# Reordering the hand-over from the adapter stage to the expert tiles on four engine queues

## Chip, cores and metric

The kernel runs on one core of one Trainium2 chip. The metric is the device time of one execution in microseconds (us); the median of the timed runs counts.

## What is computed

Two layers over 4096 tokens (8 batches of 512) with 256 channels. Layer 0 adds to x a feed-forward net whose input is a low-rank adapter of x, chosen by a language id; its activations and weights are rounded to 8 bits. Layer 1 runs a per-language adapter with a layer norm over the rows, a router with 9 experts, and the two best experts of each token:

```python
x = x + L0_ffn(L0_cond(x, ids0, lora_A, lora_B, lang_embed), clips, w_gate, w_up, w_down)
y = L1_cond(x, ids1, W1, b1, W2, b2, gamma, beta)       # adapter, residual, layer norm
probs = softmax(y @ Wr); topk_w, topk_idx = top_k(probs, 2); topk_w /= sum(topk_w)
cw[token, topk_idx] += topk_w                           # 9 experts
gate = silu(einsum('th,ehi->tei', y, Wg))
out = einsum('tei,eih,te->th', gate * einsum('th,ehi->tei', y, Wu), Wd, cw)
return x + out
```

## The kernel before

Five engines run hand-written instruction lists, each in its own order: SP (which only issues DMAs), PE (TensorE), ACT (ScalarE), DVE (VectorE) and POOL (GpSimd). They meet only at named semaphores. What an engine does next is the next call in its list; a call whose semaphore is not yet there holds up all that stands behind it on that engine. The change moves calls inside these lists.

**Front part (0 to about 190 us).** The dense feed-forward net of layer 0, then the adapter of layer 1 in 16 steps of 256 tokens (ST = 16), two to a batch `b`. Per batch DVE computes router logits (`logits`), the two choices (`first_choice`, `second_choice`, which write one-hot masks `OH`), and later, when PE has summed the masks (`rank`), the place of each token in its expert's list (`positions`) and the payload columns (`payload`, which raises the semaphore `route`). `gain` and `affine` finish the normalised rows in `pay`, and SP stores them to the DRAM table `rows` (`store_rows`). PE's `adapter_out` of a step feeds that step's `gain` (line 1243); ACT's `squares` (line 898) follows the gain, DVE's `variance` (line 1220) follows both steps' squares, and ACT's `second_weight` (line 940) is needed by `payload`. For each batch POOL turns the places into 8 one-hot tiles (`slot_hot`, lines 1672 to 1680), raising `lh`.

**Hand-over (about 190 to 262 us).** It consists of these pieces.

- `order_experts` and `first_tiles` (lines 1352 to 1374, DVE) sort the experts by their load after six batches. The result `perm` is what SP's `load_piece` (lines 456 to 464) waits for: piece n is one of the matrices Wg, Wu, Wd (n % 3) of expert n // 3 in that order, 0.7 MB each.
- A piece must be split into two fp16 halves before PE can use it: ACT `piece_sum` (948, 950), PE `piece_top` (659), DVE `piece_scale` (1379 to 1386), ACT `piece_hi` (956), DVE `piece_lo` (1394).
- The rows of the first 5 tiles (SOLO = 5) are fetched early. DVE `hot_first` (1324) and PE `slots_first` (591) find which token sits in which slot, DVE `token_rows` (1341 to 1348) writes their indices (`it` = 1), and POOL's `gather` (1699) fetches the 128 rows of a tile by an indirect DMA.
- For the other 67 tiles the same is done with `table_counts` (1408 to 1430), `table_rows` (1435 to 1447), `hot_rest` (1324, two instructions of 2304 elements a partition), PE `slots_rest` (600), `token_rows` again (`rest_rows` after the change) and `table_experts` (1450 to 1458). `table_scales` and `unscale` (1461 to 1464, 1405) fill a table of scale factors. `slots_rest` needs all eight `slot_hot` (`lh` = 8), that is also the last batch's `payload`.

**Tiles.** 72 tiles of 128 slots. In tile t: ACT `x_hi` (961), DVE `x_lo` (1471), PE `turn_rows` (668), DVE `evac_rows` (1476), PE `proj(t, 0)` (689, 12 matmuls, gate), ACT `silu` (970), PE `proj(t, 1)` (12 matmuls, up), DVE `times` (1494), ACT `h_bound` (976), DVE `h_scale` (1500 to 1504), ACT `h_hi` (980), DVE `h_lo` (1510), SP `turn_hid` (472, a DMA transpose), PE `down` (740, 17 matmuls), DVE `finish` (1519), POOL `add_rows` (1731, indirect DMA that adds into `out`). `proj(t, 1)` waits for `times(t - 1)`, since both use one PSUM region; `proj(t, 0)` waits for `silu(t - 1)` in the same way.

PE also has `keep_busy(n, bank)`: n matmuls of 128x512 whose result nobody reads.

In the lists before the change, DVE's order between the loop over batches and the loop over tiles is: gain(15), order_experts, first_tiles, variance(7), positions(6), hot_first, payload(6), affine(13), logits(7), first_choice(7), token_rows(1, ...), second_choice(7), affine(12), piece_scale(0), piece_scale(1), piece_lo(0), x_lo(0), evac_rows(0), affine(15), positions(7), payload(7), affine(14), piece_lo(1), x_lo(1), table_counts, piece_scale(2), table_rows, piece_lo(2). POOL's order there is: gather(0) to gather(4), slot_hot(6), slot_hot(7), side(0), side(1). In the loop over tiles, iteration t handles times(t - 1) and prepares tiles t + 1 and t + 2:

```python
if t == 0:
    hot_rest(0)
if t == 1:
    hot_rest(1)
if t == 2:
    token_rows(2, SOLO, TILES - SOLO, it72)
    table_experts()
if t == 3:
    table_scales()
```

Of the kernel before, what the change touches and what calls it, by code (L numbers as in the profile page):

```python
# [9 lines left out]
NB = 8  # L10
# [26 lines left out]
SOLO = 5  # L37
# [4 lines left out]
def build_program(nc, xT, id0, id1, low, clips, wg, wu, wd, W1, b1, W2, b2, gam, bet,  # L42
                  LT, Wr, Wg, Wu, Wd, out):
    ctx = ExitStack()
    with ctx:
# [236 lines left out]
        def batch(of, b):  # L282
            if 0 <= b < NB:
                of(b)
# [246 lines left out]
        def _(e):  # L531
# [11 lines left out]
            def keep_busy(n, bank):  # L543
                for _ in range(n):
                    e.matmul(ps[:, bank, :], onesb, onesb.rearrange("p (a n) -> p a n", a=1).to_broadcast([P, 4, P]), start=True, stop=True)  # L545
# [26 lines left out]
            def rank(b):  # L572
                oh = OH[:, b % 2, :]
                w.wait_ge("pos", b)
                if b == last:
                    w.wait_ge("it", 1)
                w.wait_ge("xb", XB_UN)
                w.wait_ge("oh", b + 1)
                for t in range(5):
                    o = 9 * t if t < 4 else 64  # L580
                    for u in range(min(t + 1, 4)):
                        m = e.matmul(ps[:, 6, 128 + o:128 + o + 9], tri if u == t else onesb, oh[:, 9 * u:9 * u + 9],
                                     start=(u == 0), stop=(u == min(t, 3)))
                m.then_inc(S["rk"], 1)
# [66 lines left out]
            def piece_top(n):  # L651
                w.wait_ge("hsum", 2 * n + 2)
                if n == 0:
                    w.wait_ge("relu", ST)
                else:
                    w.wait_ge("hsc", sc_after(n - 1))
                if n == 3:
                    w.wait_ge("sq", ST)
                e.matmul(top(n), onesb, col(wsb, n), start=True, stop=True).then_inc(S["htopp"], 1)
# [148 lines left out]

            for b in range(NB + 1):
                step(dense_down, 2 * b)  # L810
                if b < NB:
                    batch(rank, b - 2)
                step(adapter_out, 2 * b - 1)
                if 0 < b < NB:
                    keep_busy(3, 1)
                step(adapter_in, 2 * b)
                step(dense_down, 2 * b + 1)
                step(logits_and_rows, 2 * b)
                if b < NB:
                    keep_busy(3, 0)  # L820
                step(adapter_in, 2 * b + 1)
                step(logits_and_rows, 2 * b + 1)
                step(adapter_out, 2 * b)
            keep_busy(6, 0)
            rank(last - 1)
            keep_busy(6, 0)
            slots_first()
            piece_top(0)
            piece_top(1)
            keep_busy(10, 0)  # L830
            rank(last)
# [5 lines left out]
            for t in range(TILES + 3):  # L837
                if 0 < t < TILES:
                    proj(t, 0)
                for n in pieces(t - 1):  # L840
                    piece_top(n)
                if 0 < t < TILES - 1:
                    turn_rows(t + 1)
                if 3 <= t <= TILES:
                    down(t - 3)
                if t == 2:
                    slots_rest()
                if 0 < t < TILES:
                    proj(t, 1)
                if t == TILES - 1:  # L850
                    turn_gated_hi(TILES - 2)
                    turn_gated_lo(TILES - 2)
                if t == TILES:
                    down_hi(TILES - 2)
                    turn_gated_hi(TILES - 1)
                    down_lo(TILES - 2)
                if t == TILES + 1:
                    turn_gated_lo(TILES - 1)
                    down_hi(TILES - 1)
                    down_lo(TILES - 1)  # L860

        @block.scalar
        def _(e):
# [88 lines left out]
            def piece_hi(n):  # L952
                if n >= 6:
                    w.wait_ge("slots", 2)
                w.wait_ge("hsc", sc_after(n))
                e.activation(halves_out(n)[0], slot_in(n), ACT.Copy, scale=col(wsc, n)).then_inc(S["hhi"], 1)  # L956
# [92 lines left out]
            piece_sum(0)  # L1049
            piece_sum(1)  # L1050
            piece_hi(0)
            second_weight(last)
            x_hi(0)
            piece_hi(1)
            piece_sum(2)
            x_hi(1)
# [25 lines left out]
        def _(e):  # L1082
# [246 lines left out]
                w.wait_ge("lh", 6)  # L1329
                same_tile(hot5, q16[:, 0:48], r16[:, 0:SOLO], 48, SOLO)  # L1330

            def hot_rest(k):
                w.wait_ge("slotF", 1)
                w.wait_ge("lh", 4 * k + 4)
                same_tile(hot72[:, 32 * k:32 * k + 32, :], q16[:, 32 * k:32 * k + 32], r16, 32, TILES)

            def token_rows(k, at_, n, tmp):
                v, low_, none_, both = tmp
# [227 lines left out]
            for b in range(-1, NB):  # L1566
                step(affine, 2 * b - 3)
                step(residual, 2 * b)
                step(gain, 2 * b - 1)
                step(clip_h, 2 * b + 1)  # L1570
                batch(positions, b - 2)
                batch(variance, b - 1)
                batch(payload, b - 2)
                step(affine, 2 * b - 4)
                step(residual, 2 * b + 1)
                batch(logits, b - 1)
                batch(first_choice, b - 1)
                step(clip_h, 2 * b + 2)
                batch(second_choice, b - 1)
                step(gain, 2 * b)  # L1580
            gain(ST - 1)
            order_experts()
            first_tiles()
            variance(last)
            positions(last - 1)
            hot_first()
            payload(last - 1)
            affine(ST - 3)
            logits(last)
            first_choice(last)  # L1590
            token_rows(1, 0, SOLO, it5)
            second_choice(last)
            affine(2 * last - 2)
            piece_scale(0)
            piece_scale(1)
            piece_lo(0, (0, 1))
            x_lo(0)
            evac_rows(0)
            affine(ST - 1)
            positions(last)  # L1600
            payload(last)
            affine(ST - 2)
            piece_lo(1, (0, 1))
            x_lo(1)
            w.wait_ge("pos", NB)
            table_counts()
            piece_scale(2)
            table_rows()
            piece_lo(2, (0, 1))
            w.wait_ge("route", NB)  # L1610
            w.wait_ge("ad", ST)
            for t in range(TILES + 3):
                if 0 <= t - 1 < TILES:
                    times(t - 1)
                if t == TILES:
                    evac_gated(t - 2)
                for n in pieces(t - 3):
                    if n in split:
                        piece_lo(n, (1,))
                for n in pieces(t - 2):  # L1620
                    piece_lo(n, (0,) if n in split else (0, 1))
                if 0 <= t - 1 < TILES:
                    h_scale(t - 1)
                if t + 2 < TILES:
                    x_lo(t + 2)
                if t + 1 < TILES:
                    evac_rows(t + 1)
                if t == TILES:
                    finish(t - 3)
                if 0 <= t - 1 < TILES:  # L1630
                    h_lo(t - 1)
                if t >= 3 and t != TILES:
                    finish(t - 3)
                if t == TILES + 1:
                    evac_gated(t - 2)
                for n in pieces(t - 1):
                    piece_scale(n)
                if t == 0:
                    hot_rest(0)
                if t == 1:  # L1640
                    hot_rest(1)
                if t == 2:
                    token_rows(2, SOLO, TILES - SOLO, it72)
                    table_experts()
                if t == 3:
                    table_scales()
                for n in range(3, 3 * E):
                    if max(begin[n] + 1, 3) == t:
                        unscale(n)

        @block.gpsimd
        def _(e):
# [118 lines left out]
            for b in range(NB):  # L1771
                batch(slot_hot, b - 2)
                power(b)
            for t in range(SOLO):
                gather(t)
            slot_hot(last - 1)
            slot_hot(last)
            side(0)
            side(1)
            for t in range(TILES + 3):  # L1780
                if 2 <= t < TILES + 2:
                    weigh(t - 2)
                if 2 <= t <= 3:
                    gather(2 * t + 1)
                    gather(2 * t + 2)
                if 4 <= t < TILES - 5:
                    gather(t + 5)
                if t >= 3:
                    add_rows(t - 3)
                if t + 2 < TILES:  # L1790
                    side(t + 2)
# [61 lines left out]
```

## Time and profile before

| what | us |
|---|---|
| runs | 658.28, 661.67, 664.20 |
| median | 661.67 |
| profiled execution, its own time | 658.28 |
| its span, first to last instruction | 656.6 |
| outside the span (658.28 - 656.6) | 1.7 |
| PE busy | 602.6 (92%) |
| DVE busy | 514.8 (78%) |
| ACT busy | 440.1 (67%) |
| POOL busy | 441.8 (67%) |

Starts are counted from the first instruction of the span. "Busy" leaves out waits and the issuing of DMAs. The granted clock is a share of TensorE's 2.4 GHz: 0.50 is 1.2 GHz, 1.00 is 2.4 GHz. A label of the form `<-X` beside an idle time names what the trace takes to have ended that wait.

### The profile page before, as it was taken

The page shows a single profiled execution, that of the slowest core. Times are in us where ns is not written, and L with a number is a line of the kernel's source. Part 1 is how long each engine was busy: PE and PEld are TensorE (multiplying, and loading weights), DVE is VectorE, ACT ScalarE, POOL GpSimd, SP SyncE. Part 2 cuts the span into 40 slices and gives each one's busy share as a digit, 9 for nine tenths or more (in the row PEclk, how much of TensorE's full clock was granted, in tenths as well). Part 3 has the DMA queues.
Part 4 walks back from the last instruction along what each step waited for, and adds up shares of the span by engine and source line. Part 5 has one row for each costly group of instructions (what it writes and reads, how often), then busy time and mean ns, then how long its engine had stood idle before and what let it go on. Part 6 is the DMA issues. An engine that isn't in the chain of part 4 may idle for free.

```text
span 656.6 us, 15688 instructions
## 1 busy us (share of the span) xinstructions
PE 602.6 (92%) x4478; PEld 412.7 (63%) x4482; DVE 514.8 (78%) x1361; ACT 440.1 (67%) x744; POOL 441.8 (67%) x597
## 2 busy tenths in 40 slices
PE   7998888999994487999999999999999999999995
PEld 2343335766762265677777777777777777777774
DVE  5579995899997887888888888888776666666653
ACT  3759995998964456888787787777665444555542
POOL 4116560187885986888888888878878677666544
PEclk8979999999996798999999999999999999999998
DMA  8522001346448238999898999978996666666552
GB/s 268 205 51 87 1 0 50 97 133 211 146 134 272 90 52 183 237 194 201 179 187 164 190 165 193 198 121 111 153 162 115 112 111 109 109 111 116 100 91 33
DMA packets 149378, 89.35 MB, mean 136 GB/s; under 512 B 106788, under 2 KB 142260, under 8 KB 149300
## 3 DMA queue, kind: packets, MB, share of 16 engines
q1 hardware_dynamic: 134596, 68.77, 47.0%
q0 software_dynamic: 14080, 19.54, 18.0%
q8 instruction: 44, 0.72, 0.5%
q14 instruction: 34, 0.28, 0.1%
q10 hardware_dynamic: 624, 0.03, 0.1%
HBM read 44.68 MB, written 18.40 MB: 96 GB/s over the span
## 4 chain that ended last, share of the span: by engine, by line
PE 51%; DVE 24%; issue 8%; DMA 7%; ACT 5%; SPq 2%; POOL 2%; POOLq 1%; DVEq 0%; ACTq 0%
PE ps L689 27%; PE ps L740 14%; DMA small<-small 3%; PE ps L545 2%; DVE big L1552 2%; DVE big L1394 2%; PE ps L668 2%; DVE small L1191 2%; DVE big L1201 1%; DVE small L1265 1%; PE ps L563 1%; PE ps L540 1%; DVE small L1243 1%; DVE small L1510 1%; DMA big<-in_Wu 1%
## 5 line engine op out<-in xcount | busy, mean ns | idle before, releaser
L689 PE MATMUL ps<-big,small 128*128 x1608 | 251.7, 313 | 1.9 <-ACT small L970 1.3
L689 PEld LDWEIGHTS ps<-big,small 128*128 128x128 f16 x1608 | 156.9, 98 | 80.4 <-issue 3.8
L1731 POOL DMA_INDIRECT out<-small x67 | 107.4, 1603 | 75.5 <-DVE small L1519 73.7
L740 PE MATMUL ps<-big,small 128*128 x1105 | 131.3, 273 | 0.6 <-DMA small<-small 0.6
L740 PEld LDWEIGHTS ps<-big,small 128*128 128x128 f16 x1105 | 105.2, 98 | 12.2 <-issue 1.0
L976 ACT ACTIVATE small<-small 128x704 f16<-128x704 f32 x67 | 52.6, 785 | 77.7 <-DVE small L1494 71.6
L1510 DVE SCALAR_TENSOR_TENSOR small<-small 128x64 f16<-128x64 f32 (+1 forms) x134 | 72.6, 583 | 20.5 <-ACT small L980 14.4
L1699 POOL DMA_INDIRECT small<-rows,small x67 | 75.8, 1131 | 11.8 <-issue 10.6
L1494 DVE SCALAR_TENSOR_TENSOR small<-ps,small 128x704 f32<-128x704 f32 x67 | 63.5, 947 | 25.0 <-issue 13.2
L980 ACT ACTIVATE small<-small 128x704 f16<-128x704 f32 x67 | 59.1, 882 | 28.0 <-DVE small L1504 28.0
L1707 POOL TENSOR_SCALAR small<-small 128x1 f32<-128x1 f32 x67 | 69.7, 1040 | 0.0
L1680 POOL TENSOR_SCALAR big<-small 128x128 f16<-128x128 f32 x64 | 61.3, 971 | 0.9
L1660 POOL TENSOR_TENSOR big<-small 128x512 f32<-128x512 f32 x24 | 31.6, 1315 | 44.7 <-ACT small L1028 44.7
L970 ACT ACTIVATE small<-ps,small 128x704 f32<-128x704 f32 x67 | 55.5, 829 | 0.0
L956 ACT ACTIVATE big<-big,small 128x1408 f16<-128x1408 f32 (+1 forms) x24 | 36.0, 1500 | 27.7 <-DVE small L1383 27.7
L1394 DVE SCALAR_TENSOR_TENSOR big<-big,small 128x704 f16<-128x704 f32 (+3 forms) x45 | 45.5, 1018 | 5.0 <-ACT big L956 3.8
L545 PE MATMUL ps<-small 128*128 128x512 bf16 x151 | 43.6, 425 | 1.4 <-POOL small L1736 1.4
L948 ACT ACTIVATE big<-big 128x1408 f16<-128x1408 f32 (+1 forms) x24 | 33.6, 1401 | 7.0 <-DMA big<-in_Wg 5.2
L1666 POOL TENSOR_TENSOR small<-small 128x4 f32<-128x4 f32 x8 | 8.3, 1040 | 44.5 <-DVE small L1220 44.5
L1519 DVE TENSOR_SCALAR small<-ps,small 128x256 f32<-128x256 f32 x67 | 36.0, 537 | 1.8 <-PE ps L714 1.7
L689 PE MATMUL ps<-big 128*128 128x352 f16 x120 | 23.4, 354 | 14.8 <-DVE big L1476 7.2
L1025 ACT ACTIVATE small<-ps,small 128x512 f32<-128x512 f32 x48 | 33.7, 806 | 3.9 <-PE ps L791 2.9
(266 smaller groups left out, 1068.5 us busy)
## 6 DMA issues: line engine op xcount, KB each, us to landing
big<-in_Wg SPq DMA_DIRECT2D x8, 704.0 KB, 6.2
big<-in_Wu SPq DMA_DIRECT2D x8, 704.0 KB, 8.4
big<-in_Wd SPq DMA_DIRECT2D x8, 640.0 KB
rows<-small SPq DMA_DIRECT2D x8, 518.0 KB, 5.0
big<-in_xT SPq DMA_DIRECT2D x8, 512.0 KB, 7.0
small<-in_xT SPq DMA_DIRECT2D x16, 256.0 KB, 4.5
out<-big SPq DMA_DIRECT2D x16, 256.0 KB, 4.3
small<-rows,small POOLq DMA_INDIRECT x67
```

The source lines that it names most:

```text
L545: e.matmul(ps[:, bank, :], onesb, onesb.rearrange("p (a n) -> p a n", a=1).to_broadcast([P, 4, P]), start=True, stop=True)
L689: m = e.matmul(ps[:, 2 * j + h, 0:352], xsT_(t)[:, 2 * xp + k, :], bigh[:, bass.ds(o + (4 * j + 2 * wp + k) * I + 352 * h, 352)], start=(n ...
L740: m = e.matmul(ps[:, 7, 0:H], hTE_(t)[:, hc_, :], bigh[:, bass.ds(o + 8 * I + (6 * wp + c) * H, H)], start=(n == 0), stop=(n == len(terms) ...
L970: e.activation(hid_(t).rearrange("p (a n) -> p a n", a=2), ps[:, 0:2, 0:352], ACT.Silu, scale=factor(t, 0)).then_inc(S["sg"], 1)
L980: e.activation(hh_(t)[:, 0:I], hid_(t), ACT.Copy, scale=hc_of(t)[:, 2:3]).then_inc(S["hhi2"], 1)
L1394: m = e.scalar_tensor_tensor(lo[:, a_:b_], slot_in(n)[:, a_:b_], col(wsc, n), hi[:, a_:b_], ALU.mult, ALU.subtract)
L1494: e.scalar_tensor_tensor(v, ps[:, 2:4, 0:352], factor(t, 1), v, ALU.mult, ALU.mult).then_inc(S["hid"], 1)
L1510: m = e.scalar_tensor_tensor(hh_(t)[:, o:o + b_ - a_], hid_(t)[:, a_:b_], hc_of(t)[:, 2:3], hh_(t)[:, a_:b_], ALU.mult, ALU.subtract)
L1680: m = e.tensor_scalar(lohot[:, 8 * b + i, :], ioP, slot8[:, i:i + 1], value[:, 4 * b + i % 4:4 * b + i % 4 + 1], ALU.is_equal, ALU.mult)
L1699: e.indirect_dma_start(out=xs_(t), out_offset=None, in_=Xs[0:512 * 6, :] if t < SOLO else Xs[:, :], in_offset=bass.IndirectOffsetOnAxis(ap ...
L1707: e.tensor_scalar(w_[:, 0:1], x_[:, 258:259], slotF[:, t:t + 1], 1.0, ALU.is_equal, ALU.subtract).then_inc(S["wc"], 1)
L1731: e.indirect_dma_start(out=out[:, :], out_offset=bass.IndirectOffsetOnAxis(ap=IT[:, t:t + 1], axis=0), in_=yw_(t), in_offset=None, compute ...
```

## The change

No instruction's shape is changed and no computing instruction is added or taken away; calls are moved within the lists of PE, ACT, DVE and POOL. SP's list stays.

- PE: `rank(6)` runs ahead of `adapter_out(15)`; the two keep_busy(6, 0) become one keep_busy(12, 0); `piece_top(0)` runs ahead of `slots_first`; `slots_rest` runs after `proj(1, 1)`, where it stood ahead of `proj(2, 1)`.
- ACT: `x_hi(0)` runs ahead of `second_weight(7)`.
- DVE: `order_experts` and `first_tiles` go into the last pass of the batch loop, ahead of `logits(6)`; the list behind the loop has a new order; `table_counts`, `table_rows` and both halves of `hot_rest` run together in iteration 0 of the tile loop, `rest_rows` and `table_experts` in iteration 1, `table_scales` in iteration 2.
- POOL: `slot_hot(6)` runs ahead of the five first gathers; `gather(5)` and `gather(6)` run in iteration 1, and so on to `gather(8)` in iteration 3.

```diff
 # PE
             for b in range(NB + 1):
                 step(dense_down, 2 * b)
-                if b < NB:
-                    batch(rank, b - 2)
+                batch(rank, b - 2)
                 step(adapter_out, 2 * b - 1)
...
-            keep_busy(6, 0)
-            rank(last - 1)
-            keep_busy(6, 0)
+            keep_busy(12, 0)
+            piece_top(0)
             slots_first()
-            piece_top(0)
             piece_top(1)
...
-                if t == 2:
-                    slots_rest()
                 if 0 < t < TILES:
                     proj(t, 1)
+                if t == 1:
+                    slots_rest()
 # ACT
             piece_hi(0)
+            x_hi(0)
             second_weight(last)
-            x_hi(0)
             piece_hi(1)
 # DVE
+            def hot_rest():
                 w.wait_ge("slotF", 1)
+                w.wait_ge("lh", NB)
+                for k in range(2):
+                    same_tile(hot72[:, 32 * k:32 * k + 32, :], q16[:, 32 * k:32 * k + 32], r16, 32, TILES)
...
                 step(residual, 2 * b + 1)
+                if b == last:
+                    order_experts()
+                    first_tiles()
                 batch(logits, b - 1)
...
+            affine(ST - 3)
             gain(ST - 1)
-            order_experts()
-            first_tiles()
-            variance(last)
             positions(last - 1)
             hot_first()
+            variance(last)
             payload(last - 1)
-            affine(ST - 3)
+            affine(2 * last - 2)
+            piece_scale(0)
+            token_rows(1, 0, SOLO, it5)
             logits(last)
             first_choice(last)
-            token_rows(1, 0, SOLO, it5)
             second_choice(last)
-            affine(2 * last - 2)
-            piece_scale(0)
             piece_scale(1)
+            x_lo(0)
             piece_lo(0, (0, 1))
-            x_lo(0)
             evac_rows(0)
+            piece_lo(1, (0, 1))
+            x_lo(1)
             affine(ST - 1)
             positions(last)
             payload(last)
             affine(ST - 2)
-            piece_lo(1, (0, 1))
-            x_lo(1)
+            piece_scale(2)
             w.wait_ge("pos", NB)
-            table_counts()
-            piece_scale(2)
-            table_rows()
             piece_lo(2, (0, 1))
...
+            chunks = ((table_counts, table_rows, hot_rest), (rest_rows, table_experts), (table_scales,))
...
+                if t < len(chunks):
+                    for part in chunks[t]:
+                        part()
 # POOL
+            slot_hot(last - 1)
             for t in range(SOLO):
                 gather(t)
-            slot_hot(last - 1)
             slot_hot(last)
...
-                if 2 <= t <= 3:
-                    gather(2 * t + 1)
-                    gather(2 * t + 2)
-                if 4 <= t < TILES - 5:
+                if t == 1:
+                    gather(SOLO)
+                if 1 <= t < TILES - 5:
                     gather(t + 5)
```

## Rows read from the trace of the kernel before

**Rows 1.** The page: PE's busy time, share of the span, instructions.

```profile
PE 602.6 (92%) x4478; PEld 412.7 (63%) x4482; DVE 514.8 (78%) x1361; ACT 440.1 (67%) x744; POOL 441.8 (67%) x597
```

**Rows 2.** Stretches: length, each engine's busy us, granted clock, DMA share, GB/s.

```profile
200.00:210.00 10.00, 2.76 (x24) 1.21 (x21) 7.06 (x35) 4.89 (x8) 4.18 (x5) 0.53 1.04 324
...
262.00:656.00 394.00, 384.90 (x3080) 287.11 (x3078) 297.93 (x750) 253.93 (x422) 296.26 (x398) 0.99 0.82 144
```

**Rows 3.** Chain that ended last, 186 to 262 us: start, us, what.

```profile
189.59 0.75 DVE small L1254 x4
```

**Rows 4.** DVE timeline: start, us, instruction, [idle before <- what ended it].

```profile
193.25 0.33 DVE L1298 TENSOR_TENSOR small<-small 128x36 bf16<-128x36 f32 x1
...
195.49 0.16 DVE L1352 TENSOR_TENSOR small<-small 128x9 f32<-128x9 f32 x1
...
198.06 0.28 DVE L1220 TENSOR_SCALAR small<-small 128x4 f32<-128x4 f32 x1
...
209.14 1.68 DVE L1394 SCALAR_TENSOR_TENSOR big<-big,small 128x1408 f16<-128x1408 f32 x1 [0.46 <-issue]
...
220.95 0.16 DVE L1379 TENSOR_SCALAR small<-ps 128x1 int32<-128x1 int32 x1 [2.02 <-PE ps L659]
...
221.41 0.85 DVE L1435 TENSOR_TENSOR small<-small 128x648 f32<-128x648 f32 x1
...
225.05 1.80 DVE L1394 SCALAR_TENSOR_TENSOR big<-big,small 128x1536 f16<-128x1536 f32 x1
...
227.45 2.54 DVE L1324 TENSOR_TENSOR big<-small 128x2304 f16<-128x2304 f16 x1
229.92 0.94 DVE L1494 SCALAR_TENSOR_TENSOR big<-ps,small,big 128x704 f32<-128x704 f32 x1
...
241.90 0.21 DVE L1341 COPY small<-ps 128x67 f32<-128x67 f32 x1
...
244.59 0.95 DVE L1494 SCALAR_TENSOR_TENSOR big<-ps,small,big 128x704 f32<-128x704 f32 x1
...
249.24 0.43 DVE L1471 TENSOR_TENSOR small<-small 128x256 f16<-128x256 f32 x1 [2.22 <-ACT small L961]
...
254.47 0.93 DVE L1494 SCALAR_TENSOR_TENSOR big<-ps,small,big 128x704 f32<-128x704 f32 x1
```

**Rows 5.** ACT timeline, same columns.

```profile
194.62 0.47 ACT L898 ACTIVATE small<-ps,small 128x256 bf16<-128x256 f32 x1 [2.26 <-DVE small L1243]
...
202.55 1.38 ACT L948 ACTIVATE big<-big 128x1408 f16<-128x1408 f32 x1 [5.22 <-DMA big<-in_Wg]
...
210.97 0.42 ACT L961 ACTIVATE big<-big 128x256 f16<-128x256 f32 x1 [1.68 <-DMA big<-rows,small]
...
221.53 1.57 ACT L956 ACTIVATE big<-big,small 128x1536 f16<-128x1536 f32 x1 [6.78 <-DVE small L1383]
```

**Rows 6.** POOL timeline, same columns.

```profile
188.55 0.38 POOL L1672 TENSOR_SCALAR small<-small 128x8 f32<-128x8 f32 x1
...
189.87 6.37 POOL L1680 TENSOR_SCALAR big<-small 128x128 f16<-128x128 f32 x8
...
204.61 1.14 POOL L1699 DMA_INDIRECT big<-rows,small  x1 [5.14 <-DVE small L1348]
...
212.93 9.01 POOL L1680 TENSOR_SCALAR big<-small 128x128 f16<-128x128 f32 x8
...
243.28 1.05 POOL L1699 DMA_INDIRECT small<-rows,small  x1 [1.06 <-DVE small L1348]
```

**Rows 7.** PE timeline, same columns.

```profile
212.82 1.97 PE L689 MATMUL ps<-big 128*128 128x352 f16 x12 [0.52 <-DVE big L1476]
...
227.59 3.70 PE L689 MATMUL ps<-big 128*128 128x352 f16 x12 [6.70 <-DVE big L1476]
...
258.79 1.96 PE L689 MATMUL ps<-big,small 128*128 x12 [0.44 <-ACT big L970]
```

**Rows 8.** DMA queue of POOL's gathers, 207 to 208 us: packets, MB, share.

```profile
q0 software_dynamic: 16, 0.06, 18.1%
```

**Rows 9.** SP timeline: first weight piece issued.

```profile
198.44 0.36 SPq L459 DMA_DIRECT2D big<-in_Wg  x1
```

More of the change, by code:

```diff
@@ L1330, in hot_first, with rest_rows @@
                 same_tile(hot5, q16[:, 0:48], r16[:, 0:SOLO], 48, SOLO)
-            def hot_rest(k):
+            def hot_rest():
                 w.wait_ge("slotF", 1)
-                w.wait_ge("lh", 4 * k + 4)
-                same_tile(hot72[:, 32 * k:32 * k + 32, :], q16[:, 32 * k:32 * k + 32], r16, 32, TILES)
+                w.wait_ge("lh", NB)
+                for k in range(2):
+                    same_tile(hot72[:, 32 * k:32 * k + 32, :], q16[:, 32 * k:32 * k + 32], r16, 32, TILES)
+            def rest_rows():
+                token_rows(2, SOLO, TILES - SOLO, it72)
             def token_rows(k, at_, n, tmp):
@@ L1637, in _ @@
                     piece_scale(n)
[L1638 to L1646, printed above, removed]
+                if t < len(chunks):
+                    for part in chunks[t]:
+                        part()
                 for n in range(3, 3 * E):
-                    if max(begin[n] + 1, 3) == t:
+                    if max(begin[n] + 1, len(chunks) - 1) == t:
                         unscale(n)
```

## The prediction

> **What bounds the kernel now.** I read the page first: PE is busy 92% of the span [rows 1]. The table of stretches says where the other 8% lies. From 262 us to the end PE is busy 384.9 of 394 us at a clock of 0.99 [rows 2]: there the kernel is bound by PE's matmuls, tile after tile, and nothing waits for a fixed time of day. What the change touches lies before. Between 200 and 210 us PE is busy 2.8 of 10 us at a clock of 0.53 [rows 2]. So the end moves by as much as the moment at which PE starts to run without gaps. I take that to be proj(5, 0), at 258.79 [rows 7].
>
> What decides that moment is read from the chain of waits and DVE's timeline: up to 250 us the chain runs mostly over DVE's list, which runs in order. So I lay out DVE's new list by the old durations, and look at each wait. The marks are times(0) at 229.92, times(2) at 244.59 and times(3) at 254.47 [rows 4].
>
> **The change part by part.**
>
> *Ordering of the experts.* order_experts and first_tiles take 198.06 - 195.49 = 2.57 us [rows 4]. They now start at 189.5, where logits(6) starts today [rows 3]; perm comes 6 us earlier, and Wg is issued at about 192.5 instead of 198.44 [rows 9]. ACT waits 5.22 us for Wg today, until 202.55 [rows 5]. But logits(6) and all behind it start 2.6 us later. OH of batch 6, done at 193.58 [rows 4], comes at 196.1. PE now has rank(6) ahead of adapter_out(15), so both wait for that: rank about 0.35, adapter_out about 1.0, and gain(15) runs at 197.8 to 198.9. Today gain(15) ends at 195.6. squares (two pairs of instructions, about 2.1 us from 194.62 [rows 5]) end 3.3 us later, and with second_weight and scale_beta ACT is free at 200.7. Hence piece_sum(0) runs at 200.7, against 202.55. Of the 6 us by which the weights come earlier, ACT's queue lets through 1.9 for piece 0 and about 3.4 for piece 1.
>
> *The first rows.* This is where I see the loss. variance(7) ends at 200.3, payload(6) at 201.2. Then POOL: slot_hot(6) now stands ahead of gather(0). A slot_hot takes 189.87 + 6.37 - 188.55 = 7.7 us [rows 6]; from 201.6 it ends at 209.3. The wait chain of gather(0) adds some 0.4. So gather(0) is issued at 209.7, not at 204.61 [rows 6]. The index table it reads is ready at 205 either way. Today x_hi(0) starts 6.36 us after the issue of the gather (204.61 to 210.97 [rows 5, 6]), beside a DMA share of 1.04 [rows 2]; the first bytes of the gather queue move in 207 to 208 [rows 8], 2.4 to 3.4 us after the issue. The later gather(5) takes 243.28 to about 248.8, 5.5 us, beside a weight load. In the new kernel the weight pieces are through by 209, so the queue is nearly free. Ends: 3.3 us (bytes at once after the 2.4) and 6.4 us. I take 4.3, nearer to the row of the first bytes plus about 1 us of data and 1 us to the semaphore. That gives X = 214.0 for x_hi(0), against 210.97: +3.0 us.
>
> The Trainium skill, "DMA: Bandwidth & Descriptors", section "Anatomy of one DMA — SWDGE (gpsimd) path", gives about 2.0 us plus the bytes over 436 GB/s for a transfer issued by GpSimd, an estimate of 2.3 us for 0.13 MB. By it X would be 212.0 and the sum 2 us smaller, close to rival C. This trace does not agree: both gathers that anything waits for took 5.5 us or more.
>
> *After the rows.* From X on the order counts. x_lo(0) now stands ahead of piece_lo(0), and piece_lo(0) (1.68 us [rows 4]) ahead of evac_rows(0). DVE has no work between 209.0 (piece_scale(1)) and X, so piece_lo(0), which could run there, runs behind X. proj(0, 0) starts at X + 2.95 = 217.0. PE has been idle since about 209, and the row of a proj behind a long idle time shows 3.70 us against 1.97 at the full clock [rows 7]; I count 3.5. proj(0, 1) at X + 6.4 takes 2.0, turn_rows(1) and piece_top(2) follow, and piece_scale(2) runs at X + 8.95 = 222.95. It was 220.95 [rows 4]. DVE's other work (piece_lo(1), x_lo(1), two affine, positions, payload, 4.8 us) ends at X + 7.6 and waits. Then ACT piece_hi(2) to 225.0, DVE piece_lo(2) 225.05 to 226.8, x_hi(2), evac_rows(1) to 227.7: proj(1, 0) starts at 227.8, close to today's 227.59 [rows 7].
>
> *Tables.* Today table_counts (1.5 us) runs in the wait for piece_top(2), which still leaves 2.02 us idle, and table_rows (221.41 to 225.05, 3.65 us) beside piece_hi(2) [rows 4, 5]. In the new order these waits cover nothing, and table_counts, table_rows and both hot_rest (2.47 each [rows 4]) stand between evac_rows(1) and times(0): 1.5 + 3.65 + 4.95 = 10.1 us. hot_rest waits for lh = 8; slot_hot(7) starts at 221.2 and by the longest row (10.3 with its head) ends before 233, when DVE arrives, so that wait costs nothing. times(0) starts at 237.7, against 229.92: +7.8. proj(1, 1) waits for it, at half clock to 242.4, and slots_rest behind it ends at 244.8. DVE is through with h_lo(0) and piece_scale(3) at 242.8 and waits 2 us for slots_rest; token_rows and table_experts (241.90 to 244.59, 2.7 us [rows 4]) run to 247.6. times(1) 247.6, then table_scales and four unscale (2.2 us) inside that iteration, times(2) 254.2: +9.6.
>
> *What comes back.* Behind times(2) today's kernel has table_scales and unscale, and the wait for gather(5), issued at 243.28 [rows 6] and delaying x_lo by 2.22 [rows 4]: 9.9 us from times(2) to times(3). In the new kernel the tables are done and gather(5), issued at 246.2, lands about 252, before it is wanted at 255. That iteration takes 5.7 us. times(3) is at 259.9, against 254.47: +5.4. proj(5, 0) follows the full chain of silu and matmuls at 264.2, against 258.79: +5.4. No later wait depends on the clock on the wall, so +5.4 stays to the end.
>
> **Sum.** 658.28 + 5.4 = 663.7 for an execution like the profiled one. That one was the fastest of three, 3.4 us below the median; against the median of 661.67 the forecast is 667.1, +0.8%.
>
> **Rivals.**
>
> *A, slower still.* slot_hot(6) stretches, or gather(0) needs its long latency. The Trainium skill, "SBUF — State Buffer", section "Who interferes with whom", says that a VectorE instruction with two SBUF inputs and a GpSimd instruction that reads SBUF shut each other out for their whole length. As a mechanism of this kernel: DVE's affine(12), choices and scale steps between 201 and 209 hold up the 8 instructions of slot_hot(6). Against it speaks the row of 6.37 us for 8, with DVE about 90% busy on just such small work [rows 6]. For it speaks a slower one, 9.0 us for the same 8 instructions from 212.93 on, beside piece_lo [rows 6]. At 9.0, X is 2.6 later; with a latency of 6.4 as well, 4.7 later. Time: 669.7 to 671.8.
>
> *B, not slower.* The rows are not last. If gather(0) left POOL without waiting for slot_hot(6)'s engine time, or the eight instructions took half, X would be at most 208.6; each us of X passes on one to one, so at 208.6 the loss is gone, and DVE runs straight from piece_scale(1). Then what counts is that weights are earlier by 1.9 and 3.4 us: 661.67 less 0 to 3.4 is 658.3 to 661.7. For it: ACT's 5.22 us wait for weights is today the longest of the hand-over. Against it: POOL works in order, and the shortest row of its eight instructions is 6.37 us [rows 6].
>
> *C, the same mechanism at half size.* The gather lands with the lower end of its latency, 3.3 us (X = 213.0, -1.0), and PE keeps its full clock over the wait, so proj(0, 0) takes 2.0 and piece_scale(2) waits only for DVE's own work (-1.3). For it: the gather queue meets no weights in 210 to 214. Against it: PE is idle for 8 us before, longer than ahead of the 3.70 row. Time: 5.4 - 2.3 = +3.1, 664.8.
>
> **How the numbers follow.** Forecast 0.48 (own range 665 to 669.5), A 0.19, B 0.16, C 0.17. About 1% (6.6 us) is what a measurement of this kernel can tell from no change. Slower by more than that: A and a quarter of the forecast, 0.32. Faster by more: the part of B in which the early weights also remove the half-clock stretches, 0.07. The rest, 0.61, lies within. The range 659.5 to 671.5 holds C, the forecast and most of A and B.
>
> **What would show it.** In the new profile: Wg issued near 192.5; gather(0) issued near 209.7 behind eight L1680; ACT idle some 8 us with a releaser of the rows' DMA at L961, near 214; DVE idle near 5 us before L1471; proj(0, 0) over 3 us long; two L1324 of 2304 elements directly before the first L1494 near 237.7; L1341 of 67 columns waiting for PE L600. The forecast is wrong if gather(0) is issued before 206, if L1494 starts before 232, or if proj(5, 0) starts before 260.

## The result, and the profile after the change

The changed kernel takes 666.18 us (median of 12 runs, 663.39 to 671.31) against 660.77 (12 runs, 658.28 to 664.82). The ratio is 1.0088, 95% interval 1.0063 to 1.0113: 5.8 us slower; the two medians are 5.4 us apart. The forecast was 5.4. Single runs of 671.53, 899, 3384 and 3495 us among the experiments below count as slow and are left out of the ratios.

The page of the changed kernel: PE's busy time is what it was [rows 1].

```profile
PE 601.7 (91%) x4482; PEld 412.5 (62%) x4482; DVE 516.1 (78%) x1361; ACT 439.6 (66%) x744; POOL 439.1 (66%) x597
```

The span is 663.5 us, 6.9 more than before. Not all of it is the change. The last DVE instruction ahead of everything the change touches is residual(15). In single executions it starts up to 2.7 us apart, for reasons in the untouched front part. The DVE timelines, first before, then after:

```profile
188.73 0.87 DVE L1201 SCALAR_TENSOR_TENSOR big<-ps,small 128x256 f32<-128x256 f32 x2
```

```profile
190.06 0.88 DVE L1198 SCALAR_TENSOR_TENSOR big<-ps,small 128x256 f32<-128x256 f32 x2 [0.26 <-issue]
```

From here on I count from this instruction ("R"). The hand-over ends with proj(5, 0), whose row of before is in [rows 7]. Before, it is 258.79 - 188.73 = 70.1 us behind R; after, 265.66 - 190.06 = 75.6. That is +5.5 us, in line with the 5.8 of the timed runs. Behind that mark both profiles have 397.8 us left.

The DVE timeline of the changed kernel, with the waits that are new:

```profile
200.32 0.18 DVE L1235 COPY small<-ps 128x20 f32<-128x20 f32 x1 [0.89 <-PE ps L647]
...
206.89 0.17 DVE L1349 TENSOR_SCALAR small<-small 128x5 int32<-128x5 f32 x1
...
215.18 0.43 DVE L1472 TENSOR_TENSOR big<-big 128x256 f16<-128x256 f32 x1 [3.85 <-ACT big L958]
...
224.34 0.16 DVE L1380 TENSOR_SCALAR small<-ps 128x1 int32<-128x1 int32 x1 [2.30 <-PE ps L659]
...
226.60 1.84 DVE L1395 SCALAR_TENSOR_TENSOR big<-big,small 128x1536 f16<-128x1536 f32 x1 [1.71 <-ACT big L953]
...
234.78 5.03 DVE L1321 TENSOR_TENSOR big<-small 128x2304 f16<-128x2304 f16 x2
239.72 0.94 DVE L1495 SCALAR_TENSOR_TENSOR big<-ps,small,big 128x704 f32<-128x704 f32 x1
...
246.15 0.23 DVE L1342 COPY small<-ps 128x67 f32<-128x67 f32 x1 [1.40 <-PE ps L600]
```

Compared with [rows 4], the waits to see are 3.85 us for the first rows (before: 0.59 there), 2.30 for piece_top(2) with no table work in front of it (before: 2.02 with it), 1.71 for piece_hi(2), which table_rows used to fill, and 1.40 for slots_rest (before: none). The two instructions of hot_rest run back to back ahead of times(0) (L1495). POOL and ACT show why the rows are late (POOL first, then ACT):

```profile
205.32 6.29 POOL L1675 TENSOR_SCALAR big<-small 128x128 f16<-128x128 f32 x8
211.79 1.14 POOL L1694 DMA_INDIRECT big<-rows,small  x1 [0.18 <-POOL big L1675]
```

```profile
214.73 0.42 ACT L958 ACTIVATE big<-big 128x256 f16<-128x256 f32 x1 [7.14 <-DMA big<-rows,small]
```

The indices were ready at 207.1 (L1349), but the gather had to wait for the eight instructions of slot_hot(6), 4.7 us. PE, idle meanwhile, then runs proj(0, 0) and proj(0, 1) in 6.46 us for 24 matmuls, at a granted clock of 0.50 from 216 to 222:

```profile
217.59 6.46 PE L689 MATMUL ps<-big 128*128 128x352 f16 x24 [1.32 <-DVE big L1477]
...
240.72 3.37 PE L689 MATMUL ps<-big 128*128 128x352 f16 x12 [7.22 <-DVE big L1495]
...
265.66 1.96 PE L689 MATMUL ps<-big,small 128*128 x12 [0.15 <-issue]
```

Behind proj(5, 0) the stretch is full as before [rows 2]:

```profile
265.00:663.00 398.00, 388.54 (x3110) 289.76 (x3108) 301.78 (x758) 257.43 (x429) 301.34 (x401) 1.00 0.82 146
```

### The profile page after: what moved, and what is told of

Its sections match the earlier page's. It is cut to its first block, busy times and chain, and to the rows that moved or that the text cites. A ratio compares the mean times of both kernels' runs of the same rounds, so it can differ in the third digit from the quotient of the medians.

```text
span 663.5 us, 15695 instructions
## 1 busy us (share of the span) xinstructions
PE 601.7 (91%) x4482; PEld 412.5 (62%) x4482; DVE 516.1 (78%) x1361; ACT 439.6 (66%) x744; POOL 439.1 (66%) x597
## 4 chain that ended last, share of the span: by engine, by line
PE 60%; DVE 17%; issue 7%; DMA 6%; ACT 4%; SPq 3%; POOL 2%; POOLq 1%; DVEq 0%; ACTq 0%
PE ps L689 33%; PE ps L740 17%; DMA small<-in_xT 2%; PE ps L668 2%; DVE big L1553 2%; PE ps L545 1%; DVE small L1188 1%; DMA small<-small 1%; PE ps L800 1%; PE ps L563 1%; DVE big L1198 1%; PE ps L540 1%; DMA big<-in_low 1%; PE ps L635 1%; DVE big L1395 1%
## 5 line engine op out<-in xcount | busy, mean ns | idle before, releaser
L1694 POOL DMA_INDIRECT small<-rows,small x67 | 77.2, 1152 | 23.5 <-DVE small L1349 12.9
L1495 DVE SCALAR_TENSOR_TENSOR small<-ps,small 128x704 f32<-128x704 f32 x67 | 63.5, 948 | 24.8 <-PE ps L689 12.8
L1702 POOL TENSOR_SCALAR small<-small 128x1 f32<-128x1 f32 x67 | 71.1, 1061 | 0.0
L1675 POOL TENSOR_SCALAR big<-small 128x128 f16<-128x128 f32 x64 | 56.2, 889 | 0.9
L545 PE MATMUL ps<-small 128*128 128x512 bf16 x151 | 40.5, 402 | 1.4 <-POOL small L1731 1.4
L689 PE MATMUL ps<-big 128*128 128x352 f16 x120 | 25.2, 375 | 17.4 <-DVE big L1495 9.0
L800 PE MATMUL ps<-small 128*128 128x512 bf16 x96 | 30.1, 397 | 8.4 <-DVE big L1553 8.3
```

Of the source, the lines that this page charges most:

```text
L689: m = e.matmul(ps[:, 2 * j + h, 0:352], xsT_(t)[:, 2 * xp + k, :], bigh[:, bass.ds(o + (4 * j + 2 * wp + k) * I + 352 * h, 352)], start=(n ...
L1495: e.scalar_tensor_tensor(v, ps[:, 2:4, 0:352], factor(t, 1), v, ALU.mult, ALU.mult).then_inc(S["hid"], 1)
L1675: m = e.tensor_scalar(lohot[:, 8 * b + i, :], ioP, slot8[:, i:i + 1], value[:, 4 * b + i % 4:4 * b + i % 4 + 1], ALU.is_equal, ALU.mult)
L1694: e.indirect_dma_start(out=xs_(t), out_offset=None, in_=Xs[0:512 * 6, :] if t < SOLO else Xs[:, :], in_offset=bass.IndirectOffsetOnAxis(ap ...
L1702: e.tensor_scalar(w_[:, 0:1], x_[:, 258:259], slotF[:, t:t + 1], 1.0, ALU.is_equal, ALU.subtract).then_inc(S["wc"], 1)
```

## The experiments

Each was timed in five rounds beside the kernel before. "R to proj(5, 0)" is from each run's own profile; it leaves out what single executions differ by ahead of R and behind proj(5, 0) (397.2 to 400.1 us in the fourteen profiles). It is one profile a kernel, and has its own spread: in four runs whose lists are the same up to gather(0) (changed, tables in the waits, piece_lo(0) first, fillers) the gather is issued 20.8 to 21.7 us behind R, and in the three with the gathers first 17.6 to 18.5. So a difference of about 1 us at the mark is not shown by the mark alone.

| kernel | ratio to before, 95% | R to proj(5, 0), us |
|---|---|---|
| before | 1 | 70.1 |
| changed | 1.0088 (1.0063 to 1.0113) | 75.6 |
| changed, gathers first | 1.0077 (1.0051 to 1.0103) | 75.6 |
| changed, tables in the waits | 1.0033 (1.0007 to 1.0059) | 73.2 |
| changed, piece_lo(0) first | 1.0068 (1.0042 to 1.0094) | 74.7 |
| changed, order late | 1.0107 (1.0073 to 1.0141) | 78.3 |
| changed, gathers first, hot_rest split | 1.0070 (1.0050 to 1.0090) | 72.5 |
| the same with tables in the waits | 1.0026 (1.0009 to 1.0043) | 71.9 |
| changed, filler matmuls before the rows | 1.0077 (1.0051 to 1.0103) | 74.7 |
| changed, rank(6) behind adapter_out(15) | 1.0058 (1.0037 to 1.0079) | 74.7 |
| before, slot_hot(6) ahead of the gathers | 1.0067 (1.0040 to 1.0093) | 72.5 |
| before, order early | 1.0015 (1.0002 to 1.0027) | 70.2 |
| before, piece_lo(1) early | 0.9984 (0.9966 to 1.0002) | 69.2 |
| before, the same and token_rows early | 0.9984 (0.9961 to 1.0008) | 69.1 |

**Gathers first.**

```diff
             # POOL
-            slot_hot(last - 1)
             for t in range(SOLO):
                 gather(t)
+            slot_hot(last - 1)
             slot_hot(last)
```

> The changed kernel with one thing undone: POOL issues the five first gathers ahead of slot_hot(6) again. Theory 1 (the late first rows are one half of the loss): gather(0) is issued near 207.8 in place of 211.8 us, x_hi(0) starts near 212 in place of 214.7, and each us passes on to the end: 2 to 3 us less than the changed kernel, ratio to the kernel before 1.0045 to 1.006 (the changed kernel has 1.0088). Rival (the early ordering of the experts on DVE is what costs, rows are not last): no change, 1.0088. Rival (the rows are the whole loss): ratio 1.000.

It gave nothing by the mark at proj(5, 0) (75.6) and 0.7 us by the clock, within the error. Yet x_hi(0) came 1.3 us sooner behind R (213.00 - 189.63 = 23.4, against 214.73 - 190.06 = 24.7). The DVE timeline of this run says where that went:

```profile
234.06 5.03 DVE L1321 TENSOR_TENSOR big<-small 128x2304 f16<-128x2304 f16 x2 [1.79 <-POOL big L1675]
```

hot_rest now waits 1.79 us for the last slot_hot: POOL has the same work, and what stands second is late. So the undone edit seems masked by another edit, the merged wait for lh = 8; the next run takes that wait away. The 1.3 us, not the 2.7 expected, has its own reason: the gather was issued at 207.23, but landed only at 213.00, 5.8 us later, since the weights of pieces 3 and 4 were still moving.

**The merged wait taken away.** hot_rest split in two, hot_0 (waits for lh = 4) and hot_1 (lh = 8), the second ahead of rest_rows in iteration 1:

```diff
             # DVE, on top of the run before
-            chunks = ((table_counts, table_rows, hot_rest), (rest_rows, table_experts), (table_scales,))
+            chunks = ((table_counts, table_rows, hot_0), (hot_1, rest_rows, table_experts), (table_scales,))
```

> The changed kernel with the gathers first on POOL, and hot_rest in two calls again (the first waits for lh = 4 in iteration 0, the second for lh = 8 in iteration 1, ahead of rest_rows). Theory: in the run with the gathers first alone, x_hi(0) came 1.6 us sooner and piece_scale(2) 2.5 us sooner, but hot_rest then stood waiting for the last slot_hot; without that wait times(0) starts near 234.5, and some of it is lost again in the wait of rest_rows for slots_rest: proj(5, 0) 1.5 to 2.5 us sooner than in the changed kernel, ratio 1.005 to 1.0065. Rival (the rows' lateness has no part in it at all): 1.0077 to 1.009, as with the gathers first alone.

72.5 by the mark, 3.1 us sooner than the changed kernel; 1.2 us by the ratio (1.0070), with intervals that overlap. The mark is better than the theory, the ratio a little worse than its 1.0065. The run doesn't divide the gain between the rows and the split: the split alone, with slot_hot(6) still first, was not run, and it also takes 2.5 us of DVE work from in front of times(0). That late rows cost time by themselves is shown by the run in the kernel before, further down.

**Tables in the waits.**

```diff
             # DVE
+            w.wait_ge("pos", NB)
+            table_counts()
             piece_scale(2)
-            w.wait_ge("pos", NB)
+            table_rows()
             piece_lo(2, (0, 1))
...
-            chunks = ((table_counts, table_rows, hot_rest), (rest_rows, table_experts), (table_scales,))
+            chunks = ((hot_rest,), (rest_rows, table_experts), (table_scales,))
```

> The changed kernel with table_counts ahead of piece_scale(2) and table_rows ahead of piece_lo(2), as before the change; everything else as changed, both hot_rest in iteration 0 too. Theory 1 (the other half of the loss is DVE work taken out of the cover of two waits): table_counts (2.0 us) goes back into the wait of 2.3 us for piece_top(2), and 1.7 of the 3.6 us of table_rows into the wait for piece_hi(2): times(0) starts 3.6 us earlier, 3.6 to 5 us less at the end, ratio 1.001 to 1.0035. Rival (late rows are the whole loss; DVE has slack later): within 1 us of the changed kernel, 1.0075 to 1.0088.

2.4 us by the mark, 3.6 by the ratio: the largest single part, and the only single edit undone whose interval lies clear of the changed kernel's. times(0) starts 3.3 us sooner behind R (46.3 against 49.7; 3.6 were expected). DVE's timeline shows the wait for piece_top(2) filled (0.15 us left of 2.30), and a new one behind it: hot_rest, earlier now, waits 1.13 us for POOL.

```profile
223.85 0.16 DVE L1380 TENSOR_SCALAR small<-ps 128x1 int32<-128x1 int32 x1 [0.15 <-PE ps L659]
...
231.74 5.03 DVE L1321 TENSOR_TENSOR big<-small 128x2304 f16<-128x2304 f16 x2 [1.13 <-POOL big L1677]
```

**All three.**

> The run before with table_counts ahead of piece_scale(2) and table_rows ahead of piece_lo(2) as well. Theory: both halves add up, since the waits are on one engine's list: 2.7 us from the tables beside 1.5 to 2.5 from the rows, ratio 1.000 to 1.0025. Rival (one wait hides behind the other): no better than the run with the tables in the waits alone, 1.0033 or more.

71.9 by the mark, 1.0026 by the ratio: 3.7 to 4.1 us of the 5.5 to 5.8 are back. The two parts, 3.1 and 2.4 by the mark, do not add in full. That this run is better than the tables' run alone rests on 1.3 us of the mark; the ratios (1.0026 and 1.0033) can't be told apart, so the rival stands by the clock.

**piece_lo(0) first.**

```diff
             # DVE
-            x_lo(0)
             piece_lo(0, (0, 1))
+            x_lo(0)
             evac_rows(0)
```

> The changed kernel with piece_lo(0) ahead of x_lo(0) again, so that its 1.7 us run while DVE waits for the rows. Theory 1: evac_rows(0) and all behind it 1.6 us earlier, ratio 1.006 to 1.0068. Rival (PE's half clock in proj(0, 0) or the weights set the time of piece_scale(2)): less than 0.5 us, 1.008 to 1.0088.

0.9 us by the mark, 1.3 by the ratio. From x_hi(0) to proj(0, 0) it is now 2.05 us (215.18 to 217.23), not 2.86. That 0.8 us is the edit's: x_hi(0) itself came as late behind R as in the changed kernel (24.7). The expected 1.6 us forgot that DVE now waits 0.70 us for turn_rows(0), which piece_lo(0) had covered.

**rank(6) behind adapter_out(15).**

```diff
             # PE
-                batch(rank, b - 2)
+                if b < NB:
+                    batch(rank, b - 2)
                 step(adapter_out, 2 * b - 1)
...
+            rank(last - 1)
             keep_busy(12, 0)
```

> The changed kernel with rank(6) behind adapter_out(15) on PE again. Theory: adapter_out(15) no longer waits for DVE's choices and then runs at half clock (2.1 us); gain(15), squares, payload(6), slot_hot(6) and the first gather come about 1 us earlier, ratio 1.0065 to 1.0078. Rival (the order of these two is free): 1.0085 to 1.009, and gain(15) no earlier.

0.9 us by the mark, 2.0 by the ratio, with overlapping intervals: a gain of this edit is likely, not shown. In the changed kernel adapter_out(15) waits with PE idle for 3.82 us and then takes 2.12 us, at a clock of 0.50 from 196 to 200; here both last adapter_outs together take 2.08 us (from 193.45), at 1.00. gain(15) no longer waits and starts 9.3 us behind R, against 10.5. But in the run with piece_lo(0) first, where rank(6) was not moved, it starts at 9.5, since adapter_out(15) took 1.50 us there: of the 1.2 us, 0.2 to 1.2 can be the edit's. PE's timeline of the changed kernel:

```profile
197.78 0.52 PE L582 MATMUL ps<-small 128*128 128x9 bf16 x14 [3.82 <-DVE small L1295]
198.16 2.12 PE L647 MATMUL ps<-small 65*128 65x266 f32 x4
```

**Filler matmuls.** `keep_busy(10, 0)` between rank(7) and turn_rows(0).

> The changed kernel with ten more filler matmuls on PE between rank(7) and turn_rows(0), where it is idle for 4.3 us and then runs proj(0, 0) and proj(0, 1) for 6.5 us, partly at half clock. Theory (the half clock adds to the loss, since piece_scale(2) waits 2.3 us for PE): the 24 matmuls take 4 to 4.5 us, that wait shrinks to about 0.3, ratio 1.0055 to 1.007. Rival (the wait is covered): 1.008 to 1.009.

The 24 matmuls took 5.12 us instead of 6.46, not the 4 to 4.5 expected: the fillers (2.32 us) were over 2.05 us before turn_rows(0), and PE waited 1.53 us once more ahead of proj(0, 0). piece_scale(2) waits 0.96 us for PE, not 2.30 (0.3 expected). 0.9 us by the mark, 0.7 by the ratio, which alone would not show it.

**Ordering the experts early or late.** In the changed kernel the two calls go back behind gain(15); in the kernel before they alone go forward.

```diff
             # DVE, changed kernel ("order late")
-                if b == last:
-                    order_experts()
-                    first_tiles()
...
             gain(ST - 1)
+            order_experts()
+            first_tiles()
             positions(last - 1)
```

> The changed kernel with order_experts and first_tiles behind gain(15) again. Theory 1 (weights are not last, DVE's list is): rank(6) and adapter_out(15) come 2.6 us earlier, payload(6), slot_hot(6) and gather(0) about 2 us earlier, although the weights are issued 6 us later: 1 to 2 us less than the changed kernel, ratio 1.006 to 1.0075. Rival (the early weights are the gain that the change brings, its other parts eat it): 2 to 3.4 us more than the changed kernel, ratio 1.012 to 1.014.

> The kernel before with one edit of the change alone: order_experts and first_tiles in the last pass of the batch loop, so that perm comes 6 us earlier. Theory 2 (from the run with the late ordering: the weights and the first rows share the DMA engines, and early weights free them): gather(0) is issued as before, 204.6, but lands 1 to 2.5 us sooner, ratio 0.9965 to 0.9985. Rival (the 2.6 us by which logits, choices and gain come later on DVE are the cost of the change): ratio 1.002 to 1.004.

Here my theory of the first round fell. Late ordering made the changed kernel slower, by 2.7 us (mark) or 1.3 (ratio, with overlapping intervals); the rival's 1.012 to 1.014 was not reached either. Its gather was issued at 210.89, sooner behind R than in the changed kernel (20.7 against 21.7 us), and yet x_hi(0) came later. ACT's timeline:

```profile
217.43 0.42 ACT L958 ACTIVATE big<-big 128x256 f16<-128x256 f32 x1 [6.54 <-DMA big<-rows,small]
```

The rows took 6.54 us instead of 2.94, while the weights moved at the same time; all fourteen profiles fall into these two groups (last section). The stretch 208 to 216 us, first of the run with the late order, then of the changed kernel (the last two columns are DMA share and GB/s):

```profile
208.00:216.00 8.00, 5.68 (x61) 2.74 (x58) 4.81 (x29) 2.85 (x4) 5.96 (x7) 0.64 1.06 355
```

```profile
208.00:216.00 8.00, 1.47 (x21) 0.87 (x19) 3.70 (x19) 1.27 (x3) 6.91 (x9) 0.81 0.51 176
```

In the kernel before, early ordering brought the rows in at most 3.15 us (208.50 to 211.65, ACT was busy until then) instead of 6.36, but nothing at the end (70.2, ratio 1.0015, where neither the theory nor the rival had it). gather(0) was issued 1.2 us later behind R (17.1 against 15.9), as ordering had filled the time in which variance(7) waits for squares, and without it that wait is open (L1220). x_hi(0) still came 2.0 us sooner behind R (20.3 against 22.2), and this was lost on PE: turn_rows(0) stood behind ten filler matmuls and rank(7), so that evac_rows(0) (L1476) waited 2.2 us, and proj(0, 0) started 24.9 us behind R against 24.1. DVE's waits (what waited, for what: us in total, times, longest), then PE's fillers:

```profile
DVE big L1476 <- PE ps L668: 2.2, 1, 2.2
...
DVE small L1220 <- ACT small L898: 1.2, 1, 1.2
```

```profile
210.15 4.43 PE L545 MATMUL ps<-small 128*128 128x512 bf16 x10
```

That the fillers were what held it up was not run.

**slot_hot(6) ahead of the gathers, in the kernel before.** The reverse of the first edit.

> The kernel before with one edit of the change alone: slot_hot(6) ahead of the five first gathers on POOL. Theory 1: gather(0) is issued near 208 in place of 204.6 us, and since pieces 3 and 4 are then still moving, its latency stays near 6 us: x_hi(0) 3 us later, the end 2 to 3 us later, ratio 1.003 to 1.0045. Rival (the lesson of the run with the gathers first: whichever of the two stands second on POOL is missed, so the order is worth nothing): within 1 us, 0.9985 to 1.0015.

2.4 us by the mark, 4.4 by the ratio (5 runs, 2.6 to 6.1): this edit alone costs what was expected or more. gather(0) was issued 19.4 us behind R against 15.9, and x_hi(0) started at 215.16, 26.1 us behind R against 22.2.

**Two tries at a better kernel.** In the kernel before, DVE's order behind evac_rows(0) becomes positions(7), payload(7), piece_lo(1), x_lo(1), affine(15), affine(14). The second try also puts token_rows of the 67 tiles ahead of h_scale(1).

> The kernel before with DVE's order behind evac_rows(0) changed: positions(7), payload(7), piece_lo(1), x_lo(1), affine(15), affine(14), so that piece_lo(1) comes 1.6 us earlier and route(8) 0.8 us earlier. Theory (DVE's list and the short loop from piece_lo(1) over proj(0, 1) and piece_top(2) to piece_scale(2) set the pace): PE's wait of 2.4 us ahead of proj(0, 1) shrinks, piece_scale(2) comes 2 to 2.8 us earlier, ratio 0.996 to 0.9985. Rival (the last slot_hot on POOL or the first rows are what is waited for in the end): 0.9995 to 1.001.

> The kernel before with the order of the first of these four runs and with token_rows of the 67 tiles ahead of h_scale(1) in iteration 2, so that gather(5) is issued 2.6 us earlier. Theory: the wait of DVE and ACT for the rows of tile 5 (2.2 us) goes as well, ratio 0.9935 to 0.996. Rival (h_scale, h_hi and silu, 1 us later by that, take its place): no better than the first of these runs.

The first brings 0.9 us by the mark, within its spread; its ratio of 0.9984 reaches 1.0002, so it isn't clear of no change. PE's wait ahead of proj(0, 1) did shrink, from 2.42 to 0.71 us. The second adds nothing. The indices of tile 5 were ready at 240.3, 50.4 us behind R against 54.3, but POOL was still at work on the side calls behind slot_hot(7), and issued gather(5) at 243.42 after 0.15 us of idleness (53.5 us behind R, against 54.6); DVE waits 2.7 us for these rows, where it waited 2.2. My rival forecast the outcome, but named the wrong engine.

No kernel of this study beats the kernel before beyond doubt.

## Why the prediction was right

All marks of the prediction count in the clock of the kernel before; those of the changed kernel are shifted here by 1.33 us (190.06 - 188.73).

| mark | forecast | measured | of before |
|---|---|---|---|
| gather(0) issued | 209.7 | 210.5 | 204.61 |
| its latency | 4.3 | 2.9 | 6.4 |
| x_hi(0) | 214.0 | 213.4 | 210.97 |
| proj(0, 0) and proj(0, 1), PE time | 5.5 | 6.5 | 5.2 |
| piece_scale(2) | 222.95 | 223.0 | 220.95 |
| times(0) | 237.7 | 238.4 | 229.92 |
| times(1) | 247.6 | 247.5 | 237.50 |
| times(2) | 254.2 | 254.1 | 244.59 |
| times(3) | 259.9 | 259.9 | 254.47 |
| proj(5, 0) | 264.2 | 264.3 | 258.79 |

The agreement to 0.1 us at the last marks is partly luck: several terms were mis-sized, and the errors cancel.

- *The bound.* That the end moves by as much as proj(5, 0) held: +5.5 at that mark, +5.8 timed.
- *The first rows.* Right in its mechanism: the run that made this edit alone in the kernel before lost 2.4 us at the mark and 4.4 by the ratio. Two terms were mis-sized and offset each other. The latency was 2.94 us, not 4.3 and below my lower end of 3.3, which I had read from a busy queue. And gather(0) was issued 0.8 us later than I had it: I gave adapter_out(15) 1.0 us, and it took 2.12 at half clock. The Trainium skill, "DMA: Bandwidth & Descriptors", section "Anatomy of one DMA — SWDGE (gpsimd) path", by which I had estimated 2.3 us, was nearer to 2.94 than my 4.3. I wrote that the trace did not agree; the trace of before had no gather that anything waited for while the weights stood still.
- *Half clock.* I counted 5.5 us for the 24 matmuls, with the second 12 at the full clock; it was 6.46, with a clock of 0.50 over 216 to 222. This and the early rows (x_hi(0) 0.6 us sooner) cancel: piece_scale(2) came as forecast.
- *Tables.* Right: the waits that table_counts and table_rows had filled are open, and the run that fills them again brings 2.4 to 3.6 us. table_counts and table_rows took 5.6 us, not 5.15, and piece_lo(2) came 0.2 us late, so times(0) was 0.7 us late. The wait of rest_rows for slots_rest was 1.40, not 2 us, and that cancels it.
- *hot_rest's wait for lh = 8* cost nothing in the changed kernel, as the prediction said: the last slot_hot ended at 230.6, DVE came at 234.8. One run that brings DVE there earlier (tables) and one that puts slot_hot(6) and slot_hot(7) behind the gathers make it a wait of 1.1 and 1.8 us.
- *Early ordering.* I priced it by ACT's queue (1.9 and 3.4 us; it was 0.9 and 2.8, as ACT came free 0.9 us later than I had it). The prediction does count on the weights being through when the gather is issued, but gives the ordering no credit for it. Without it the change cost 2.7 us more by the mark. Rival B, in which the early weights win, has this much truth; its own bound, x_hi(0) at 208.6, does not follow from its conditions, since half of slot_hot's time would take off 3.2 us and give 210.8.
- *Rival A* had slot_hot(6) stretched by DVE. It took 6.29 us for the eight instructions, as in the row of 6.37 [rows 6]. Beside long DVE instructions with two SBUF inputs the same eight took 9.0 us and, in other runs, up to 10.97. The rule of the Trainium skill, "SBUF — State Buffer", section "Who interferes with whom", that the prediction cites agrees there; beside DVE's small work, much of it with two SBUF inputs too, the eight lost next to nothing.

What is shown of the loss: gathers, split and tables undone together bring back 3.7 us of 5.5 at the mark and 4.1 of 5.8 by the ratio. For the rest there are two candidates, rank(6) and piece_lo(0), with 0.9 us each at the mark. Their sum with the 3.7 is 5.5, but each is within the spread of the mark, they were measured in separate runs, and that they add was not run.

## What to carry to other kernels

On an engine that works through a list in order, the worth of a call's place is the wait it fills: write down each wait of the bounding engine and what stands in front of it before moving anything, because a call moved out of a wait costs up to the wait that it had filled (here 5.6 us of table work, moved out of waits of 4.0 us, cost 3.3 us at times(0) and 2.4 at the mark), and a call moved ahead of a transfer's issue delays it by what is left of the call when the transfer could have gone (here 4.7 us). Undo edits in pairs when one engine (here POOL) serves two readers, since undoing one can move the wait to the other. And price early loads by what they clear from the queue of the next transfer too, not by their own arrival alone.

## What the runs showed of the hardware

- A gather of 128 rows of 1036 bytes issued by POOL reached its reader 2.86 to 2.94 us after the issue in four profiles in which the weight loads had passed (3.98 in a fifth, at most 3.15 in a sixth), and 4.8 to 6.8 us in the eight in which they were still moving.
- The same eight slot_hot instructions on POOL took 6.25 to 6.97 us (7.85 in one case) where no piece_lo or hot_rest of DVE was under way before the last of them, and 7.65 to 10.97 us where one or two were. The time is lost in single instructions: of slot_hot(7) in the changed kernel seven took 0.79 to 0.81 us and one 2.36, which began 0.06 us behind piece_lo(2), 1.84 us long on DVE. In the kernel before, the one of 3.08 us overlaps piece_lo(1) (1.67), and those of 2.36 and 2.90 overlap piece_lo(2) (1.80) and hot_rest (2.54). No run changed the DVE instruction alone.
- Four f32 matmuls of 266 columns took 2.12 us at a granted clock of 0.50, after PE had been idle for 3.82 us and had run 14 short matmuls; eight in a row took 2.08 at 1.00.
